# Spare bf16 products on TensorE in three stages of a four-layer graph network kernel

## The reference

```
L0: s_i, s_j = xl @ W_att[:128], xl @ W_att[128:]        # xl = h @ W_lin + b_lin, 4 heads
    alpha = softmax over equal src of leaky(s_i[src] + s_j[dst] + b_att)
    out   = segment_sum(alpha * xl[src], dst)
L1: xj  = segment_sum((edge_attr_64 @ Wdesc.T) * ssp(xa @ Wj.T + bj)[dst], src), then dense residual layers
L2: em  = relu(layernorm([h[src], h[dst]] @ msg_w + msg_b)) * edge_weight; segment_sum over dst; gated update
L3: W   = ssp(edge_attr_50 @ mlp_w1.T + b1) @ mlp_w2.T + b2, scaled by a cosine cutoff
    agg = segment_sum(W * (h @ lin1.T)[dst], src); x + ssp(agg @ lin2.T + b)
```

## Time and profile before

| | |
|---|---|
| time, median of 3 runs | 8158.88 us (8157.78 to 8176.24) |
| profiled execution: time / span | 8096.3 us / 8094.5 us |
| TensorE clock granted over the span, mean | 0.69 of full speed |
| PE busy | 4727.6 us (58%) in 24982 matmul records |
| DVE / ACT / POOL busy | 54% / 32% / 52% |
| messages of layer 0 (L1203 first to L1254 last) | 1794 to 3080 us |
| edges of layer 1 | 3564 to 4945 us |
| edges of layer 3 | 6672 to 8050 us |

### The profile page before, as it was taken

How to read it: one execution, slowest core, us unless ns; L and a number is a source line. 1 busy time by engine, 2 the same in 40 slices (tenths; PEclk the granted TensorE clock), 3 DMA queues, 4 the chain that set the end, 5 groups by cost and what they waited for, 6 DMA issues and landing times. The chain is left out here.

```text
span 8094.5 us, 101922 instructions
## 1 busy us (share of the span) xinstructions
PE 4727.6 (58%) x24982; PEld 3600.8 (44%) x24982; DVE 4359.0 (54%) x14429; ACT 2596.5 (32%) x7267; POOL 4171.4 (52%) x4980
## 2 busy tenths in 40 slices
PE   7667776503433444635555556666666657777777
PEld 5445554303333334524444444344444445555555
DVE  8556555443333336753333337756666664555556
ACT  1434443202222325840000005633333343333333
POOL 1556555526666664455555550066666615555552
PEclk9677677655556658965555558877777766666667
DMA  1333333391111115512222220022222212222221
GB/s 55 105 109 120 114 114 108 97 49 45 45 44 45 45 46 131 145 42 58 57 59 59 58 58 12 20 66 66 65 66 65 66 35 56 54 53 55 54 55 42
DMA packets 834363, 533.65 MB, mean 66 GB/s; under 512 B 588596, under 2 KB 741000, under 8 KB 833416
## 3 DMA queue, kind: packets, MB, share of 16 engines
q1 hardware_dynamic: 702152, 261.57, 14.7%
q0 software_dynamic: 131648, 265.56, 11.7%
HBM read 399.11 MB, written 127.68 MB: 65 GB/s over the span
## 5 line engine op out<-in xcount | busy, mean ns | idle before, releaser
L1388 POOL DMA_INDIRECT l2e_rows<-l_rows,columns x832 | 796.8, 958 | 826.2 <-POOLq L226 366.0
L1388 POOL DMA_INDIRECT spare<-l_rows,k_dst_of x784 | 740.1, 944 | 730.1 <-DVE l3e_prod L2433 297.3
L1388 POOL DMA_INDIRECT table<-l_rows,k_dst_of x784 | 740.6, 945 | 643.9 <-DVE l1e_prod L1626 356.5
L1254 POOL DMA_INDIRECT dst_rows<-l0d_out,l0d_idx x832 | 828.5, 996 | 457.6 <-issue 249.6
L851 POOL DMA_INDIRECT src_records<-sort_rec,sort_idx x784 | 769.6, 982 | 571.3 <-issue 310.8
L906 DVE TENSOR_TENSOR spare<-spare,l1e_pR 128x128 f32 x832 | 238.4, 287 | 881.0 <-DMA l0m_rows<-dst_rows 636.3
L1596 PE MATMUL l1e_pG<-k_weights,table 64*128 64x128 f32 x1568 | 237.9, 454 | 650.3 <-ACT table L1617 514.6
L1213 PE MATMUL l0d_pX<-table,l0d_ohT 128*128 x1664 | 395.7, 406 | 349.0 <-ACT l0d_ohT L1231 172.5
L2366 PE MATMUL l3e_pH<-table,k_weights 50*128 50x256 f32 x784 | 375.7, 572 | 305.2 <-DMA const_lin<-src_lin 292.3
L1213 PEld LDWEIGHTS l0d_pX<-table,l0d_ohT 128*128 128x128 f32 x1664 | 337.1, 284 | 397.6 <-issue 397.6
L1596 PEld LDWEIGHTS l1e_pG<-k_weights,table 64*128 64x128 f32 x1568 | 181.2, 317 | 722.9 <-ACT table L1617 562.4
(11 more groups left out here) (419 smaller groups left out, 13183.7 us busy)
## 6 DMA issues: line engine op xcount, KB each, us to landing
l0m_rows<-dst_rows SPq DMA_DIRECT2D x196, 264.0 KB, 2.9
sort_rows<-lo_rows SPq DMA_DIRECT2D x196, 256.0 KB
sort_rec<-rec SPq DMA_DIRECT2D x98, 472.0 KB
l2e_lrow<-dst_local SPq DMA_DIRECT2D x208, 128.0 KB
table<-src_records SPq DMA_DIRECT2D x196, 128.0 KB
table<-src_records SPq DMA_DIRECT2D x196, 100.0 KB
dst_rows<-l0d_out,l0d_idx POOLq DMA_INDIRECT x832
l2e_rows<-l_rows,columns POOLq DMA_INDIRECT x832
```

Source lines behind the costliest of these rows:

```text
L1254: e.indirect_dma_start(kn.by_dst[:, :], bass.IndirectOffsetOnAxis(ap=r["idx"][:, st.quad, j:j + 1], axis=0), r["out"][:, st.quad, j, :], N ...
L1388: e.indirect_dma_start(r["rows"][:, i % ring, j, 0:width], None, table[:, :], bass.IndirectOffsetOnAxis(ap=columns[:, i * G + j:i * G + j ...
```

## The change

A helper issues n products of the bf16 identity with itself (repeated along the columns) into a PSUM region that nothing reads. They wait for no semaphore and raise none. The phases call it as one more stage of TensorE's stream: in l0d three products of 512 columns after `pick` and three after `turn`, in l1e four of 256 columns after `mults` and four after `turn_rec`, in l3e three of 256 columns after `even`. In l0d they write a new bank, in the other two a part of the transposes' banks that was free.

```diff
+def keep_busy(kn, e, out, n):
+    for _ in range(n):
+        e.matmul(out.rearrange("p (j c) -> p j c", c=P), kn.identb[:, :],
+                 kn.identb[:, None, :].to_broadcast([P, out.shape[-1] // P, P]), start=True, stop=True, skip_group_check=True)
...
-            run_steps(e, ch, [(pick, 3), (turn, 1)], STEPS, 0)
+            def extra(st):
+                keep_busy(kn, e, r["pZ"][:, :], 3)
+            run_steps(e, ch, [(pick, 3), (extra, 3), (turn, 1), (extra, 1)], STEPS, 0)
...
-            run_steps(e, ch, [(mults, 1), (add, 3, 1, STEPS), (turn_rec, 0)], TSTEPS, 0)
+            def extra(st):
+                keep_busy(kn, e, r["pD"][:, 1 - st.par, 2 * P:4 * P], 4)
+            run_steps(e, ch, [(mults, 1), (extra, 1), (add, 3, 1, STEPS), (turn_rec, 0), (extra, 0)], TSTEPS, 0)
...
-            run_steps(e, ch, [(add, 7, 1, STEPS), (filt, 5), (even, 2), (turn_rec, 0), (odd, 2)], TSTEPS, 0)
+            def extra(st):
+                keep_busy(kn, e, r["pD"][:, st.par, 2 * P:4 * P], 3)
+            run_steps(e, ch, [(add, 7, 1, STEPS), (filt, 5), (even, 2), (extra, 2), (turn_rec, 0), (odd, 2)], TSTEPS, 0)
```

More of the change, by code:

```diff
@@ L1260, in build @@
         return dict(sync=sync, vector=vector, tensor=tensor, scalar=scalar, gpsimd=gpsimd)
-    phase(kn, "l0d", build, psums=[("pT", [P, 2, 2 * G, P], BF16), ("pX", [P, 2, G, 2 * P], F32)],
+    phase(kn, "l0d", build, psums=[("pT", [P, 2, 2 * G, P], BF16), ("pX", [P, 2, G, 2 * P], F32), ("pZ", [P, BANK], F32)],
                sbufs=[("oh", [P, 4, G, P], BF16), ("ohT", [P, 4, G, P], F32),
```

## The result

The changed kernel takes **8326.06 us** (median of 4 runs, 8311.52 to 8340.2) against 8158.33 us for the kernel before (4 runs, 8130.3 to 8176.24): a ratio of 1.0216, interval 1.0193 to 1.0239. It is slower; 8101 us were forecast, and the time lies above the range too. The profiled execution took 8323.7 us, span 8320.4 us.

A forecast was written before the change was run, and what follows sets the result against it. The prediction took TensorE's low clock, and POOL's waits between bursts, to bound the indirect-DMA stages. Gains of 29 (l1e) and 45 (l3e) less 16 lost (l0d) gave -58 us: 8158.9 to 8101 us, own range 8027 to 8138, 8-in-10 range 7980 to 8260.

The forecast's parts named there:

- The l0d term: In l0d, spare products delay each burst's first step, so 4.1 instead of 4.45 steps per POOL wait: 16 us lost.
- The price of 0.45 us per product: TensorE's column-streaming time for one 512-column product at half clock; 0.22 us at full clock.
- l1e, -29 us: In l1e, a higher clock speeds bursts, raising 3.04 steps per POOL wait to 3.3: 29 us gained.
- l3e, -45 us: In l3e, a higher clock raises 2.58 steps per POOL wait to 3.0: 45 us gained.
- The first rival: In l1e and l3e, TensorE does not set the pace; faster steps only lengthen pauses: same, 8159 us, chance 0.24.
- The restart, 0 us: After a pause, the way to POOL's next gather still runs at half clock, so nothing was counted.
- The second rival: Spare products run at half clock, costing l1e 62 us and l0d 40 us: slower, 8260 us, chance 0.27.
- The third: Pauses come from TensorE's clock or idleness, so POOL's waits in l1e, l3e and l0d halve: 7720 us, chance 0.08.
- a change in l2e: Sign that the forecast is wrong: l2e, which has no spare products, changes; no size given.

The follow-up runs named there:

- set 1: Four kernels on one chip with pauses: kernel before again (median 8116.92 us), then spare products in l0d, l1e or l3e alone (1.0122, 0.9944, 1.0023).
- set 3: Four kernels on one chip with pauses, kernel before at 8155.54 us: whole change again (1.0175), and three smaller versions in l0d alone (1.0156, 1.0035, 1.0139).
- six narrow ones: Changed kernel with products in l0d alone, six per step of 128 columns instead of 512: 8280.49 us (1.0156) with pauses, 6604.56 us (1.0008) without.
- one and one: Changed kernel with products in l0d alone, one of 512 columns behind the picks, one behind the transposes: 1.0035 with pauses, 1.001 without.
- sets 4 and 5: Edits of the changed kernel on two chips without pauses, including plain stores for l0d's scatters (6105.99 to 6118.32 us); kernel before 6591.08 and 6588.60 us.

## Why the prediction was wrong

**The l0d term is the step that failed**, mis-sized from 16 us to 114 to 143. The prediction put it: "One step per burst comes 2.7 us late, half of POOL's 5.07; I take 0.35 step off the 4.45: 3.97 / 4.1 = 0.97 us". The steps per wait came out about right (133 / 32 = 4.2 with l0d alone, 135 / 36 = 3.8 in the repeat of the change, 135 / 35 = 3.9 in the result over waits of more than 0.6 us), but 3.97 us was not a constant. The wait itself grew to 7.0 us (224.0 / 32), so the waiting per step was 1.68 us. The price of 0.45 us per product, from the earlier trace rows, was also beside the point: the run with 128 columns cost nearly the same, and a product of 512 columns takes 0.27 us once the clock is up (three in 0.81 us at 2450.23 of the timeline). So the columns that TensorE streams in a burst are not what costs; the loss shows up in the waits.

**Behind it stands a sentence that should have been a bound**: "Nothing in this trace tells me what the pause waits for [...] and I treat it as given". An unexplained wait that TensorE's own signals sit in is not given when one adds instructions to TensorE. The range had no end for it; by an estimate from the nearest row, the whole length of a pause (7.6 us) once per burst would have been 7.6 / 4.45 x 208 = 355 us, and the loss would have been inside. The 3.97 us was a mean of unlike waits besides: 16 of the 33 over 0.6 us lie between 3 and 4 us, 9 over 5 us, while 34 of the 35 in the changed kernel lie between 6 and 7.

**l1e, -29 us.** The stage is 16 us shorter in the result and 27 to 31 us in set 1, which fits in size; in set 3 it is 1353 us with products and 1352 to 1358 without: nothing; and nothing without pauses. So the gain is shown in set 1 alone. By the profile's count there are 147 / 59 = 2.5 steps per wait of 4.5 us, where 3.3 steps per wait of 5.74 were forecast, and 1.81 us of waiting per step against 1.89 before and 1.74 in the forecast. That count mixes two kinds. Of POOL's idle stretches over 4 us, the kernel before has 47 in its window, the result 46, the repeat of the change 42, the kernel with l1e alone 36 (146 to 150 steps each): where the stage gained most, the long waits became rarer, as forecast, but short ones of 0.6 to 3 us came in between (6 before, 53 with l1e alone), which the forecast didn't have.

**l3e, -45 us.** No gain. The clock reached 0.72, not 0.8; without pauses the same products bring it to 0.94. By the profile's count 145 / 68 = 2.1 steps per wait came instead of 3.0. Over idle stretches of more than 0.6 us waits did become rarer (95 before, 82 now), but longer (3.1 us each before, 3.6 now), and their sum stayed (293 and 295 us): the constant length of a wait fails here as in l0d. The stage is 24 us longer in the result, 13 to 21 in set 3 (1396 against 1375.5, 1376 and 1383), and the run with l3e alone shows no difference. The first rival, that the pace is not TensorE's, describes l3e better than the forecast, and on the chips without pauses it holds for both stages, with POOL's gather every 900 / 715 = 1.26 us as the whole pace.

**The restart, 0 us**, holds: the picks behind the pause still run at 2.25 us.

**The second rival** has the right sign and the wrong mechanism. It was to decide at a clock under 0.7 in l0d and l1e; the clock is 0.73 and 0.74 and the loss is there. Its price for l0d was 40 us. That its 8260 us came nearest is luck.

**The third**, that pauses go once TensorE is kept busy, is refuted: in l0d the waits grow, and no stage lost half of them.

**The sort's 117 us and l2e's -14** were to be a sign against the forecast ("a change in l2e"). They are most likely no effect of the change: all kernels of set 3 have them (1458 to 1467 and 1266 to 1269 us), also the one that is 27 us over the kernel before. But the kernel before was not profiled there, so this is argued, not shown.

**Shown:** products in l0d alone bring most of the loss (1.0122 in set 1; in set 3 the six narrow ones 1.0156, against 1.0175 for the whole change); it is not the streamed columns; it comes as longer waits of POOL with about the same number of pauses; it comes only where there are pauses, since without them the products that were run (in l0d six narrow ones, one and one, or three of the six at a time) cost at most 0.1%, 0.2% by the intervals. **Open:** what a pause is, and why more instructions of TensorE change its pattern. That every stage with POOL's indirect DMAs has them and l0m does not, and that the long ones of l1e end 2.5 to 3.1 us after POOL's last issue, speaks for those DMAs holding up the other engines' instructions and signals, but the run that was to show it met chips without pauses. Loading of program code is no candidate for most of them, by the queues above. Open as well is whether it is the place behind the picks or the number of three that switches the pattern; three behind the transposes was never run where there are pauses. And as each set had one chip at one time, whether the pauses belong to a chip or to its state at the time is open too.

## What to carry to other kernels

Raising TensorE's clock was worth nothing in stages whose pace another engine sets (l1e and l3e of sets 4 and 5), and that engine's waits tell: with 5.0 us of POOL's issue in a 6.1 to 6.9 us step, only the waits between were to be won. Where an engine waits in a way the profile doesn't explain, an edit that adds instructions to it should have at least the whole unexplained wait in its range. A mean of waits hides which kinds there are; list them before one is taken for constant. And time a marginal change on more than one chip: here much the same edit costs 1 to 2% in two sets and nothing in three. Of the versions tried, products in l1e alone are the best (0.9944, then 1.0 on a chip without pauses), and not worth relying on.

## What the runs showed of the hardware that was not expected

- **The time of this kernel differs by a quarter from one set to another**, each on a chip of its own. The kernel before took 8117 and 8156 us in two, 6589, 6591 and 6601 us in three. l0m has 350.4 to 350.9 us in all of them and the dense layers between l1e and l2e about 209; the sort has 1329 to 1474 us in the one kind and 1006 to 1013 in the other, l1e 1345 to 1376 and 1010 to 1012, with and without products. One scatter or gather takes POOL the same 1.25 to 1.27 us on both.
- **In a pause TensorE crawls rather than stops**: its transposes, 0.10 us apart in a burst, start 0.7 to 1.1 us apart, and spare products, which wait for nothing, up to 2.1 us; ACT starts 7.6 us (l1e) and 11.6 us (l0d) after the last thing that it waits for.
- **A rise of the clock without a gain**: l3e at 0.94 instead of 0.79 has the same 1007 us.
